# Attention pipeline of a fused transformer kernel: a copy put behind the exponential, query splits in other steps, the last tile joined a step earlier

## What is computed

```
x = x + 0.5 * _L0_ffn_ref(_layernorm(x), ...);  x = x + _L0_attn_ref(_layernorm(x), ...);  ...
x = x + 0.5 * _L2_ffn_ref(_layernorm(x), ...)   # has attention inside, and runs twice
...
scores = jnp.einsum('bqhd,bkhd->bhqk', q, k) / np.float32(np.sqrt(HEAD_DIM))
scores = jnp.where(causal[None, None], scores, jnp.float32(-1e+30))
attn = jax.nn.softmax(scores, -1)
o = jnp.einsum('bhqk,bkhd->bqhd', attn, v)
```

## Time and profile before

| | us |
|---|---|
| median of 3 runs | 3817.97 (3817.18 to 3822.41) |
| the profiled execution | 3819.36 |
| its span, first to last instruction | 3817.3 |
| PE busy in it | 3310.2 (87%) |
| DVE, ACT, POOL busy | 2474.8, 1965.0, 1693.1 |
| attention of layer 0 | about 124 to 384 |
| the two attentions of layer 2 | about 1062 to 1723 and 2511 to 3176 |

### The profile page before, as it was taken

One profiled execution on the slowest core, in us unless ns is written; L12 is line 12 of the kernel. 1 busy time (PEld: TensorE's weight loads), 2 busy tenths in 40 slices (PEclk: granted clock), 3 DMA queues, 4 the chain that ended last, 5 costly groups with the idle time before them and its releaser, 6 DMA issues. The chain is left out here.

```text
span 3817.3 us, 55139 instructions
## 1 busy us (share of the span) xinstructions
PE 3310.2 (87%) x16736; PEld 2550.3 (67%) x16736; DVE 2474.8 (65%) x4877; ACT 1965.0 (51%) x3957; POOL 1693.1 (44%) x1293
## 2 busy tenths in 40 slices
PE   5798698479898989988995999789889987998979
PEld 4566576148566666666883899666666666886767
DVE  4687554865487878875557565477778875555554
ACT  3787433334376767764333333266667774334333
POOL 1666211742366666752212555376666662221111
PEclk8899899899899999999998999799999998999989
DMA  2000231333101111103320000110111102332232
GB/s 75 22 31 2 73 109 58 132 102 118 57 25 28 30 28 27 27 4 116 110 83 26 1 1 1 40 27 25 25 28 30 30 9 90 112 108 83 73 95 75
DMA packets 81186, 204.05 MB, mean 53 GB/s; under 512 B 17179, under 2 KB 20379, under 8 KB 80662
## 3 DMA queue, kind: packets, MB, share of 16 engines
q1 hardware_dynamic: 80774, 200.74, 16.9%
q10 hardware_dynamic: 144, 0.07, 0.0%
HBM read 170.86 MB, written 4.69 MB: 46 GB/s over the span
## 5 line engine op out<-in xcount | busy, mean ns | idle before, releaser
L1257 POOL TENSOR_TENSOR probs<-probs,row_inverse 128x640 f32<-128x640 f32 (+7 forms) x640 | 737.6, 1158 | 539.3 <-DVE row_inverse L1283 528.9
L549 PE MATMUL psUp<-xnT_part,weights_part 128*128 128x512 f32 x3456 | 832.6, 390 | 3.7 <-DVE hidden L702 2.5
L549 PEld LDWEIGHTS psUp<-xnT_part,weights_part 128*128 128x128 f32 x3456 | 649.8, 188 | 141.1 <-issue 3.2
L526 POOL TENSOR_TENSOR weights_part<-weights,weights_part 128x768 fp32r<-128x768 f32 x136 | 251.0, 1849 | 1006.6 <-ACT weights_part L605 1006.6
L1271 DVE TENSOR_REDUCE neg_max<-psS 128x1 f32<-128x640 f32 (+7 forms) x640 | 477.1, 746 | 146.6 <-PE psS L1162 145.0
L1298 DVE TENSOR_TENSOR probsT_part<-psT,probsT_part 128x512 fp32r<-128x512 f32 (+1 forms) x960 | 502.9, 551 | 92.0 <-ACT probsT_part L1240 80.6
L1240 ACT ACTIVATE probsT_part<-psT 128x512 fp32r<-128x512 f32 (+1 forms) x960 | 436.4, 491 | 215.9 <-PE psT L1174 212.6
L1224 ACT ACTIVATE probs<-psS,neg_max 128x640 f32<-128x640 f32 (+7 forms) x640 | 475.5, 743 | 102.7 <-DVE neg_max L1271 84.0
L1158 PE MATMUL psS<-k_part,q_parts 128*128 128x512 f32 (+1 forms) x960 | 414.7, 432 | 113.3 <-ACT probs L1224 74.5
L1174 PE MATMUL psT<-ident,probs 128*128 128x128 f32 x2880 | 444.8, 279 | 39.0 <-POOL probs L1257 30.4
L559 PE MATMUL psDown<-hidden_part,weights_part 128*128 128x512 f32 x1728 | 448.9, 397 | 32.2 <-DVE hidden_part L722 32.2
(11 more groups left out here) (315 smaller groups left out, 4841.0 us busy)
## 6 DMA issues: line engine op xcount, KB each, us to landing
gates<-gate_rows SPq DMA_DIRECT2D x136, 512.0 KB, 4.0
weights<-in_l_ffn SPq DMA_DIRECT2D x148, 384.0 KB, 4.4
qk_swapped<-qk_raw SPq DMA_DIRECT2D x384, 64.0 KB, 2.0
bc_broadcast<-bc_rows SPq DMA_DIRECT2D x32, 512.0 KB, 4.4
w_group<-in_l_wgroup SPq DMA_DIRECT2D x16, 384.0 KB, 3.2
q_whole<-q_steps SPq DMA_DIRECT2D x32, 128.0 KB
w_o_group<-in_l_wo SPq DMA_DIRECT2D x16, 256.0 KB, 3.2
rope<-in_l_rope SPq DMA_DIRECT2D x2, 1024.0 KB, 5.4
```

The lines of the kernel that those rows point to most:

```text
L526: nc.gpsimd.tensor_tensor(w[1][:, j, :], wt[:, j, :], w[0][:, j, :].bitcast(F32), ALU.subtract).then_inc(w_split, 1)
L549: last = nc.tensor.matmul(psU[:, u % 2, g, :], wp[:, j, g * D + k * P:g * D + (k + 1) * P], xp[:, k, cols(half)], start=n == 0, stop=n == ...
L1257: self.nc.gpsimd.tensor_tensor(self.p[:, n % 4, 0:w], self.p[:, n % 4, 0:w], self.rinv[:, at:at + 1].to_broadcast([P, w]), ALU.mult).then_ ...
```

## The change

ACT's step now issues the exponential of unit s+7 first and the join's copy behind it. Which steps join is decided by a new function: 3, 7, ..., 27 as before, and 30 in place of 31. For that, tile 0's single block is multiplied in the quad's second step (29) in place of its third. POOL's splits of query pieces move, and in layer 0 the roundings and the split of the first keys too. The diff, without the lines that only lose blanks:

```
+    def joins(self, s):
+        return s == 30 or (s > 0 and s % 4 == 3 and s < 31)
...
-            lo, hi = r * blocks // 3, (r + 1) * blocks // 3
+            lo, hi = (r // 2 if r != 1 else 0, (r + 1) // 2) if blocks == 1 else (
+                r * blocks // 3, (r + 1) * blocks // 3)
...
-            if r == 2:
+            if hi == blocks and lo < hi:
                 done.then_inc(self.valued, 1)
...
         def step(g, s, last):
-            if s % 4 == 3 and s > 0:
+            exp(g, s + 7, last)
+            if self.joins(s):
                 act.wait_ge(self.valued, NT * g + s // 4 + 1)
                 act.wait_ge(self.kept, NT * g + s // 4 + 1)
                 nc.scalar.activation(self.shift[:], self.psO[64:64 + self.dv, :], ACT.Copy).then_inc(self.shifted, 1)
-            exp(g, s + 7, last)
...
             maximum(g, s + 8, last)
-            if s % 4 == 3 and s > 0:
+            if self.joins(s):
                 dve.wait_ge(self.shifted, NT * g + s // 4 + 1)
...
     ROUND_AT = {6: (0,), 8: (1,), 10: (2,), 12: (3,), 15: (4,), 18: (5,)}
-    SPLIT_AT = {7: 0, 11: 2, 14: 3, 17: 4, 20: 5}
+    SPLIT_AT = {7: 0, 14: 2, 15: 3, 22: 4, 24: 5}
     FIRST_KEYS_AT = 10
...
-    ROUND_AT = {14: (0, 1), 16: (2,), 18: (3,), 20: (4,), 22: (5,)}
-    SPLIT_AT = {15: 0, 17: 2, 19: 3, 21: 4, 23: 5}
-    FIRST_KEYS_AT = 15
+    ROUND_AT = {4: (0, 1), 6: (2,), 12: (3,), 20: (4,), 22: (5,)}
+    SPLIT_AT = {6: 0, 8: 2, 14: 3, 22: 4, 24: 5}
+    FIRST_KEYS_AT = 6
```

## The result

The changed kernel takes 3797.02 us (median of 5 runs, 3794.17 to 3797.79) against 3817.97: a ratio of 0.9945, 95% interval 0.9933 to 0.9957. It is 21 us faster, where 47 were forecast. The time lies inside the range, near the 3798 of rival (a), but that is luck: the runs put 17 to 19 of the missing 26 us in layer 0, where no rival had looked, and only the rest in layer 2, where rival (a) applies.

A forecast was written before the change was run, and what follows sets the result against it. PE, busy 87% of the span, was taken as the bound, so gains come only from its idle time or clock; 27.4 + 4.8 + 14.0 + 1.5 = 47.7 us off 3819.4, median 1.4 lower, gave 3771, range 3754 to 3800.

The forecast's parts named there:

- rival (a): Layer 2's groups: DVE, next engine behind PE, takes half the gain back, leaving 20 us, to 3798; chance 0.15.
- Part 1: Layer 2, splits out of the wide tile's steps: values of step 24 start 1.96 us earlier a group, 27.4 us.
- Part 2: Layer 2, clock falls after the 1.96 us wait vanish in 8 of 14 groups, 0.6 each, 4.8 us.
- part 3: Exponential ahead of the join's copy: values at steps 4, 8, 12 and 16 start no earlier, 0 us.
- part 4: End of layer 2's groups, last join in step 30: last projection starts 1.0 us earlier a group, 14.0 us.
- part 5: Layer 0, roundings and key splits moved: net gain 0.5 us a group, 1.5 us; bounds -2 and +2.5 a group.
- in layer 0 ACT idle before L1846 for a load: Layer 0: one of the signs listed as showing the prediction wrong; no size given.
- PE keeps about 0.55: Layer 2, step 20: scores' 0.81 us wait for an exponential behind the join's copy shrinks, PE keeping about 0.55 us.
- Rival (b): Loop jumps: the half-rate clock after them goes as well, 4 x 2.8 = 11 us more, to 3760; chance 0.08.
- (c): Joins: DVE waits for the later copy, delaying the next values; 0.8 us mean delay costs 80, to 3850; chance 0.06.

The follow-up runs named there:

- l2_splits_only: The kernel before with only layer 2's SPLIT_AT changed, its splits moved out of the wide tile's steps: 3792.82 us.
- exp_first_only: The kernel before with only the step's exponential written ahead of the join's copy: 3820.47 us.
- no_exp_first: The changed kernel with layer 0's tables put back and the exponential written behind the join's copy again: 3779.17 us.
- last_join_only: The kernel before with only the last join moved into step 30, with the narrow tile's values one step earlier: 3808.43 us.
- l0_tables_only: The kernel before with only layer 0's three tables (roundings, splits, first keys) changed: 3834.66 us.
- l0_tables_back: The changed kernel with layer 0's three tables (roundings, splits, first keys) put back as they were: 3779.10 us.
- l0_tables_later: The changed kernel with layer 0's roundings starting in step 8, first split and first keys in step 10: 3779.77 us.
- loads_on_all_engines: The changed kernel with layer 0's staged rows laid out in DRAM so each load reads one contiguous 128 KB block: 3770.18 us.

## Why the prediction was wrong, step by step

| step | forecast us | measured | by |
|---|---|---|---|
| parts 1 and 2, splits of layer 2 with the clock | 32.2 | 26.3 | l2_splits_only |
| part 3, exponential first | 0 | -1.6, and 0 in the whole | exp_first_only, no_exp_first |
| part 4, last join (measured with layer 0's) | 14.0 | 10.7 | last_join_only |
| part 5, layer 0's tables | 1.5 | -15.5 alone, -17.9 in the whole | l0_tables_only, l0_tables_back |
| sum | 47.7 | 19.9 by single parts, 21 by the kernel | |

**Part 5 failed, at one sentence**: "The loads of the next group end at 199.28 + 1.38 + 1.7 = 202.4 now; ACT wants them at 201.0 in step 4. The store ahead of them starts with the last join, some 1.7 us earlier, so they land about in time." The 1.7 us that I put behind the last issue was not a duration of these loads, and no run shows it: they drain at some 105 GB/s, and the last of them lands 15 us after the first issue and 8 after the last. The trace of before held the answer. Its windows in layer 0's second group:

```profile
200.00:204.00 4.00, 3.98 (x28) 3.13 (x27) 3.65 (x11) 3.37 (x11) 2.95 (x3) 1.00 0.27 109
204.00:206.00 2.00, 2.00 (x13) 1.46 (x12) 1.95 (x6) 1.66 (x4) 1.23 (x2) 1.00 0.26 107
206.00:208.00 2.00, 1.71 (x10) 1.16 (x10) 1.88 (x7) 1.69 (x7) 0.47 (x2) 1.00 0.22 88
208.00:210.00 2.00, 2.00 (x11) 1.55 (x12) 1.39 (x3) 1.48 (x3) 1.30 (x2) 1.00 0.01 4
```

The DMA engines are at work until close to 208, not 202.4. ACT wanted the keys at 220.7, so the time did not show as a wait anywhere. Read from there, the rounding in step 4 would have waited some 7 us less the 1.7 to 4 by which the store comes earlier, in each of the groups that load ahead, and the half-rate clock that follows such a gap. The sign of my whole part, and a bound of -2 us a group, hung on a landing that I had not read. I had named the sign of it ("in layer 0 ACT idle before L1846 for a load"), but given it no place among the rivals. The gains that this part set against the cost did not show either: layer 0's groups with the last join alone take 67.5 as before, where 0.4 was counted, and with the wide tile free and no wait (l0_tables_later) the time is that of the old tables.

**Part 1 was right in its mechanism**, down to the single split of step 20, and mis-sized by 0.36 us a group. The values of step 24 start 64.0 us into the group with the splits alone, 65.4 before, 1.4 earlier; PE's row with the splits alone shows the rest:

```profile
1203.81 1.19 PE L1194 MATMUL psO<-probsT_part,v_parts 128*128 128x512 f32 x4 [0.93 <-DVE probsT_part L1298]
```

The second parts come 0.93 after PE is ready, where 0.72 stood before. The term that failed is "PE keeps about 0.55" at step 20, which the exponential put first should have given. In the changed kernel the scores' wait there did fall, from 0.81 to 0.21, but a new one of 0.67 stands right behind it, before the output product, whose bank DVE's second parts must empty. PE starts that product 56.0 us into the group, where it was 55.8 before. The wait at step 24 is 1.35. The two rows before, and then those of the changed kernel:

```profile
2648.41 0.38 PE L1158 MATMUL psS<-k_part,q_parts 128*128 128x256 f32 x1 [0.81 <-ACT probs L1224]
...
2649.97 1.12 PE L1643 MATMUL psT<-w_o_group,oT 128*128 128x256 f32 x4
```

```profile
1206.45 0.39 PE L1152 MATMUL psS<-k_part,q_parts 128*128 128x256 f32 x1 [0.21 <-ACT probs L1219]
...
1208.62 1.12 PE L1627 MATMUL psT<-w_o_group,oT 128*128 128x256 f32 x4 [0.67 <-DVE probsT_part L1293]
...
1216.73 1.19 PE L1189 MATMUL psO<-probsT_part,v_parts 128*128 128x512 f32 x4 [1.35 <-DVE probsT_part L1293]
```

This is what rival (a) describes, DVE as the next engine, but it took some 6 to 11 us back, not the 28 that (a) assumed. **Part 2 was right** in its place and price (0.66 against 0.6 a fall). **Part 3 was right** as a sum; that jump groups lose 1.2 us of clock and layer 0 gains 0.6 a group was in none of it. **Part 4** was mis-sized by half. Two things made it so. DVE's idle 0.37 us at step 29, which the sum takes away, is still there, at 0.38, although the scores of step 28 no longer wait. And the output product stands behind the last transposes, which themselves wait for the second parts that now stand behind the join. From the second parts of step 29 to the output product it was 4.34 us before and is 3.89 now, 0.45 less where 1.0 was forecast (changed kernel, end of a group, DVE and PE):

```profile
1229.23 0.89 DVE L1293 TENSOR_TENSOR probsT_part<-psT,probsT_part 128x512 fp32r<-128x512 f32 x2 [0.38 <-ACT probsT_part L1235]
...
1232.85 0.33 PE L1168 MATMUL psT<-ident,probs 128*128 128x128 f32 x1 [1.47 <-DVE probsT_part L1293]
1233.12 1.13 PE L1627 MATMUL psT<-w_o_group,oT 128*128 128x256 f32 x4
```

The parts add up within the noise: alone they give 19.9, together 21. Without layer 0's tables the changed kernel gains 40.0 against 35.4 by single parts and 46.2 forecast. The forecast's last step also rounds 3770.3 to 3771, which changes nothing. Rival (b) did not come (the falls at the jumps stayed), nor (c): DVE's joins waited 14.7 us for 160 copies in all, under 0.1 each. That loads_on_all_engines ends at 3770 where 3771 was forecast is mostly chance: it wins 8.6 us at layer 0's start, about what parts 1 and 4 fell short.

## What to carry to other kernels

Before work is moved ahead of a wait that is hidden today, find out when its data are really there: from the DMA's busy share and GB/s until they drop to zero, not from the last issue. The last transfer of a batch lands when the batch has drained, and if the drain leaves three quarters of the DMA engines idle, the shape of the transfers is the first thing to change. A wait that shows nowhere has a margin, and the margin is what an edit of this kind spends.

## What was not expected of the hardware

Ten loads of 128 KB each drained at 105 GB/s with the DMA engines 0.26 busy when their DRAM side was four blocks of 8 rows, and at 242 GB/s (0.82 busy) as one block of 32 rows; SP's issues took 0.8 us each in the first form (6.39 for eight) and 0.56 in the second (4.51 for eight). One gap of 6 us of PE costs more than itself: the granted clock was 0.50 for some 3 us of work behind it. Behind the loop's jumps the clock was low for some 3.3 us in two groups and for some 6.6 in two others of one and the same profile, and the length of PE's gap does not order them: 2.58 and 2.83 us with the short fall, 2.47 and 3.05 with the long one. With only ACT's order changed it was 6.6 in all four, behind gaps of 2.58 to 3.01. No row here explains which of the two comes. DVE's rotation with both inputs in SBUF ended 0.55 us behind the GpSimd instruction that it overlapped, and took 0.68 without one.
